# A decoder kernel's delta rule: query products made by GpSimd, VectorE's preparation in another order, first mixture's masked biases ahead of the sum

## What is computed

```python
for e in range(N_EXPERTS):
    h = jax.nn.relu(x @ W1[e] + b1[e])
    y = h @ W2[e] + b2[e]
    ff_out = ff_out + jnp.where((expert_idx == e)[..., None], y, 0.0)
return _layer_norm(x + ff_out, ln2_g, ln2_b)
```

```python
S = a_[..., None, None] * S
pred = jnp.einsum('bhkv,bhk->bhv', S, k_)
S = S + k_[..., :, None] * (b_[..., None] * (v_ - pred))[..., None, :]
o = jnp.einsum('bhkv,bhk->bhv', S, q_)
```

## Time and profile before

| | |
|---|---|
| median of 3 runs | 1845.26 us (1844.14 to 1848.06) |
| the profiled execution | 1845.25 us, span 1843.4 us |
| busy share of the span | TensorE 90%, VectorE 69%, ScalarE 52%, GpSimd 17% |
| mean granted TensorE clock | 0.957 of full speed |
| delta rule's preparation from k-hat to the scan | 1077.5 to 1127.4 us of the span |
| the scan | 1127.4 to 1311.5 us |

### The profile page before, as it was taken

The page is one execution under the profiler, slowest core; times in us unless marked ns, Lnnn a source line. Parts: engine busy times, 40 slices in busy tenths (PEclk is TensorE's granted clock), DMA queues, the critical chain, the costliest instruction groups (busy, mean ns, idle before and its releaser), DMA issues.

```text
span 1843.4 us, 24921 instructions
## 1 busy us (share of the span) xinstructions
PE 1653.6 (90%) x8074; PEld 736.0 (40%) x8074; DVE 1271.4 (69%) x2994; ACT 949.4 (52%) x2053; POOL 304.5 (17%) x465
## 2 busy tenths in 40 slices
PE   7899999999999989999899988444798899999998
PEld 3355455545544432222244331222443355444443
DVE  7576666767667768888565578999666677762423
ACT  3565556556645516666633566333236366664333
POOL 1000000000001021121277200000000222114443
PEclk9999999999999989999999999777799799999999
DMA  4000000000000220240000000000100512100000
GB/s 193 1 1 1 1 1 1 1 1 1 1 1 21 55 59 23 73 116 2 1 0 1 0 1 1 1 1 1 69 1 1 147 55 73 32 2 1 1 0 23
DMA packets 19806, 44.36 MB, mean 24 GB/s; under 512 B 3872, under 2 KB 13024, under 8 KB 18912
## 3 DMA queue, kind: packets, MB, share of 16 engines
q1 hardware_dynamic: 19200, 42.39, 7.6%
q10 hardware_dynamic: 480, 0.39, 0.1%
HBM read 32.74 MB, written 9.44 MB: 23 GB/s over the span
## 4 chain that ended last, share of the span: by engine, by line
PE 75%; DVE 16%; ACT 5%; issue 3%; POOL 1%; DMA 0%; ACTq 0%; POOLq 0%; SPq 0%; DVEq 0%
PE ps L675 8%; PE ps L639 8%; PE ps L653 6%; PE ps L1226 6%; PE ps L1264 5%; PE ps L1112 5%; PE ps L1699 3%; PE ps L1700 3%; PE ps L596 3%; PE ps L1596 3%; PE ps L1612 3%; PE ps L1707 3%; DVE arena L2063 2%; PE ps L684 2%; DVE arena L2050 2%
## 5 line engine op out<-in xcount | busy, mean ns | idle before, releaser
L1390 DVE TENSOR_REDUCE stat<-ps 128x1 f32<-128x512 f32 (+3 forms) x512 | 279.1, 581 | 86.6 <-PE ps L1116 43.0
L1321 ACT ACTIVATE arena<-ps 128x512 f32<-128x512 f32 (+3 forms) x512 | 247.1, 515 | 154.3 <-PE ps L1264 83.3
L826 DVE TENSOR_REDUCE stat<-ps 128x1 f32<-128x544 f32 x256 | 173.4, 719 | 163.0 <-PE ps L639 163.0
L777 ACT ACTIVATE arena<-ps,stat 128x544 f32<-128x544 f32 x256 | 180.7, 711 | 201.9 <-DVE stat L826 201.9
L1264 PE MATMUL ps<-arena 75*128 75x512 bf16 (+1 forms) x480 | 163.1, 344 | 11.7 <-ACT arena L1321 9.5
L1112 PE MATMUL ps<-arena 72*128 72x128 bf16 (+1 forms) x480 | 163.0, 348 | 8.0 <-DVE stat L1390 7.8
L675 PE MATMUL ps<-arena 128*64 128x512 f32 (+1 forms) x640 | 159.2, 609 | 4.7 <-DVE arena L845 3.3
L639 PE MATMUL ps<-arena 64*128 64x272 f32 x1024 | 152.1, 415 | 5.1 <-ACT arena L777 4.3
L785 ACT COPY arena<-ps 128x512 f32<-128x512 f32 x256 | 137.3, 594 | 15.5 <-PE ps L653 15.5
L653 PEld LDWEIGHTS ps<-wA_sb,arena 128*128 128x128 f32 x1024 | 115.1, 142 | 70.1 <-issue 68.9
L653 PE MATMUL ps<-wA_sb,arena 128*128 128x128 f32 x1024 | 138.3, 278 | 0.0
(11 more groups left out here) (391 smaller groups left out, 2775.2 us busy)
## 6 DMA issues: line engine op xcount, KB each, us to landing
arena<-b_parts SPq DMA_DIRECT2D x180, 96.0 KB
b_parts<-arena SPq DMA_DIRECT2D x64, 128.0 KB, 1.9
reg<-wM_dram SPq DMA_DIRECT2D x1, 3072.0 KB, 10.0
reg<-wB_dram SPq DMA_DIRECT2D x1, 2048.0 KB, 12.4
reg<-wM_dram SPq DMA_DIRECT2D x1, 2048.0 KB, 16.7
reg<-wD_dram SPq DMA_DIRECT2D x1, 1817.0 KB, 10.7
wF_sb<-wF_dram SPq DMA_DIRECT2D x1, 1476.0 KB, 19.8
reg<-b_parts SPq DMA_DIRECT2D x12, 96.0 KB
```

Of the source, the lines that this page charges most:

```text
L777: e.activation(prob_of(P, r).rearrange("p (a k) -> p a k", a=2), score_banks(r), ACT.Exp, bias=x_neg[:, at_:at_ + 1], accum_out=x_sums[:, ...
L826: e.tensor_reduce(x_neg[:, n % 4:n % 4 + 1], score_banks(r), AX.XY, ALU.max, negate=True).then_inc(sem("max_done"), 1)
L1321: e.activation(p_t[:, m % 8, q0:T], ps[:, S1 + m % S2, q0:T], ACT.Exp).then_inc(exp_done, 1)
L1390: e.tensor_reduce(nm[:, G % 2, u // 4, u % 4:u % 4 + 1], ps[:, step % S1, 0:keys(u)], AX.X, ALU.max, negate=True).then_inc(max_done, 1)
```

## The change

In the first mixture the four mask times bias additions come before the addition of the PSUM bank; they wait for the batch's last `up` instead of its last `down`.

In the preparation `g_ke`, `g_gq`, `g_pq[0]` and the query's six products for s = 1 to 3 are made by GpSimd (semaphore `b4_made`), which makes `g_ke` when k-hat is there and the others when q-hat is. VectorE forms `g_u` ahead of `g_z`, and q-hat behind the first of the three z and k pairs. The dots stand before the third `g_ke` pick (`KE_FIRST = 2`). `neg_delta` and the scratch of the solve get places of their own (`delta_flat`), so that k-hat and the places of the solve aren't overwritten. CB becomes 8: the `terms` buffers hold half as many blocks, and GpSimd fills 16 chunks instead of 8. VectorE waits for the last of GpSimd's products before it writes the part of `hist` that lies over alpha's second row (step 15).

```diff
--- before.py
+++ after.py
@@ -34,7 +34,7 @@
 PV_AT = 7
 BL = 4
 NB = T // BL
-CB = 16
+CB = 8
 NCB = NB // CB
 OUT = ((0, 32), (32, 32), (64, 32), (96, 16), (112, 16))
 OUT_OPS = 2 * 4 + BL
@@ -1634,15 +1634,13 @@
 
             def moe_dve(e):
                 def total(b):
+                    e.wait_ge(sem("moe_up"), (b + 1) * NI)
+                    e.wait_ge(sem("masks"), b + 1)
+                    for ex in range(E0):
+                        link(e, e.scalar_tensor_tensor(out=x_aux[:, b, :], in0=mask[:, b % 2, ex, :], scalar=v("f_b2", ex),
+                                                       in1=x_aux[:, b, :], op0=ALU.mult, op1=ALU.add))
                     e.wait_ge(sem("moe_down"), (b + 1) * NI)
-                    e.wait_ge(sem("masks"), b + 1)
-                    link(e, e.tensor_tensor(x_aux[:, b, :], ps[:, 4 + b % 2, :], x_aux[:, b, :], ALU.add))
-                    for ex in range(E0):
-                        i = e.scalar_tensor_tensor(out=x_aux[:, b, :], in0=mask[:, b % 2, ex, :],
-                                                   scalar=v("f_b2", ex), in1=x_aux[:, b, :], op0=ALU.mult, op1=ALU.add)
-                        if ex < E0 - 1:
-                            link(e, i)
-                    i.then_inc(sem("b3_sum"), 1)
+                    e.tensor_tensor(x_aux[:, b, :], ps[:, 4 + b % 2, :], x_aux[:, b, :], ALU.add).then_inc(sem("b3_sum"), 1)
                 masks(e, 1)
                 early_parts["last_total"](e)
                 early_parts["square"](e, B - 1)
@@ -1761,6 +1759,8 @@
             rank1 = slack[:, 0:64 * (BL + 1)].rearrange("p (a j d l) -> p a j d l", a=2, j=4, l=BL + 1)
             gamma = slack[:, 64 * (BL + 1):]
             g_k, g_q = c(B * T), c(B * T)
+            delta_flat = c(B * T)
+            neg_delta = delta_flat.rearrange("p (n i j) -> p n i j", i=BL, j=4)
             y = y_flat.rearrange("p (t w) -> p t w", w=12)
             k_end = k_end_flat.rearrange("p (t d) -> p t d", d=HD)
             hist = hist_flat.rearrange("p (n j d) -> p n j d", j=4, d=HD)
@@ -1770,7 +1770,7 @@
             M = B * NB
             flat = lambda x: x.rearrange("p b t -> p (b t)")
             g_alpha, g_beta = hist_flat[:, 0:BL * M], hist_flat[:, BL * M:2 * BL * M]
-            g_z, g_tmp = terms_flat[:, 0:BL * M], terms_flat[:, BL * M:BL * M + 3 * M]
+            g_z, g_tmp = terms_flat[:, 0:BL * M], delta_flat[:, 0:3 * M]
             g_pk, k_sq = y_flat[:, 0:6 * M], y_flat[:, 6 * M:10 * M]
             q_sq, g_to_end = k_end_flat[:, 0:B * T], k_end_flat[:, B * T:2 * B * T]
             qk = c(10 * M)
@@ -1785,7 +1785,6 @@
             def qk_of(s_):
                 return qk[:, PAIR0[s_] * M:(PAIR0[s_] + BL - s_) * M].rearrange("p (i b n) -> p b n i", i=BL - s_, b=B)
             q_wide = [x.rearrange("p b (n i) -> p b n i", i=BL) for x in (x_aux, cent)]
-            neg_delta = g_k.rearrange("p (n i j) -> p n i j", i=BL, j=4)
             o_prod = reg2[:, 0:8 * M].rearrange("p (a b t) -> p a b t", a=8, b=B)
             o_own = reg2[:, 8 * M:12 * M].rearrange("p (s b n i) -> p s b n i", s=BL, b=B, i=BL)
             PADW = CTAPS - 1
@@ -1798,10 +1797,11 @@
             PK0 = (None, 0, 3, 5)
             DOT0 = (0, 3, 5)
             PEB = 2
-            KE_FIRST = 5
+            KE_FIRST = 2
+            MADE = {x: n_ + 1 for n_, x in enumerate(("ke", "gq", "q0", "s1", "q1", "s2", "q2", "s3", "q3"))}
             GAMMA, KE, WW, UU, QK, GQ = 0, 1, 9, 17, 21, 31
             PICKS = 39
-            READY = {x: n_ + 1 for n_, x in enumerate(("gamma", "ke", "gq", "q0", "w", "u", "q1", "q2", "q3"))}
+            READY = {x: n_ + 1 for n_, x in enumerate(("gamma", "w", "u"))}
 
             def by_m(x, n_):
                 return x[:, 0:n_ * M].rearrange("p (i m) -> p i m", i=n_)
@@ -1865,7 +1865,7 @@
                     return lambda b: split_i(x)[:, :, b, :]
                 pick_k = [wt["pick_k"][:, d * 32:d * 32 + 32] for d in range(HD)]
                 pick_v = [wt["pick_v"][:, j * 32:j * 32 + 32] for j in range(4)]
-                e.wait_ge(sem("b4_ready"), READY["ke"])
+                e.wait_ge(sem("b4_made"), MADE["ke"])
                 e.wait_ge(sem("b4_ln"), 2 * B)
                 pick(GAMMA, pick_k[0], lambda b: split_i(g_gamma)[:, BL - 1, b, :])
                 for d in range(HD):
@@ -1889,7 +1889,7 @@
                     e.wait_ge(sem("b4_picked"), g - 1)
                     e.matmul(ps[:, 6 + g % 2, :], matrix, rhs, start=True, stop=True).then_inc(sem("b4_pick"), 1)
                 for s_ in range(BL):
-                    e.wait_ge(sem("b4_ready"), READY[f"q{s_}"])
+                    e.wait_ge(sem("b4_made"), MADE[f"q{s_}"])
                     for i in range(BL - s_):
                         wide(QK + PAIR0[s_] + i, wt["head_one"], g_pq[s_][:, i * M:i * M + M])
                 for a in range(2):
@@ -1981,13 +1981,11 @@
                     e.tensor_tensor(split_i(g_k)[:, :, b, :], tokens_by_i(ps[:, b:b + 1, :])[:, :, 0, :],
                                     split_i(r_k)[:, :, b, :], ALU.mult).then_inc(sem("b4_khat"), 1)
                 e.wait_ge(sem("b4_khat"), B)
-                e.wait_ge(sem("b4_ready"), READY["gamma"])
-                e.tensor_tensor(g_ke, g_k, g_to_end, ALU.mult).then_inc(sem("b4_ready"), 1)
                 e.wait_ge(sem("b4_act_read"), 2)
-                link(e, e.tensor_tensor(g_z, g_k, g_beta, ALU.mult))
                 e.wait_ge(sem("b4_proj"), 4 * B)
                 e.scalar_tensor_tensor(out=split_i(g_u), in0=tokens_by_i(ps[:, B:2 * B, :]), scalar=-1.0,
                                        in1=split_i(g_beta), op0=ALU.mult, op1=ALU.mult).then_inc(sem("b4_dve_read"), 1)
+                link(e, e.tensor_tensor(g_z, g_k, g_beta, ALU.mult))
                 e.wait_ge(sem("b4_ready"), READY["gamma"])
                 link(e, e.tensor_tensor(g_w, g_z, g_gamma, ALU.mult))
                 for s_ in range(1, BL):
@@ -1997,13 +1995,10 @@
                     w = (BL - s_) * M
                     e.tensor_tensor(g_pk[:, PK0[s_] * M:PK0[s_] * M + w], g_z[:, s_ * M:], g_k[:, 0:w],
                                     ALU.mult).then_inc(sem("b4_prod"), 1)
-                e.wait_ge(sem("b4_rlen"), 2 * B)
-                e.tensor_tensor(split_i(g_q), tokens_by_i(ps[:, 0:B, :]),
-                                split_i(r_q), ALU.mult).then_inc(sem("b4_dve_read"), 1)
-                e.wait_ge(sem("b4_dve_read"), 2)
-                e.wait_ge(sem("b4_ready"), READY["ke"])
-                e.tensor_tensor(g_gq, g_q, g_gamma, ALU.mult).then_inc(sem("b4_ready"), 1)
-                e.tensor_tensor(g_pq[0], g_q, g_k, ALU.mult).then_inc(sem("b4_ready"), 1)
+                    if s_ == 1:
+                        e.wait_ge(sem("b4_rlen"), 2 * B)
+                        e.tensor_tensor(split_i(g_q), tokens_by_i(ps[:, 0:B, :]),
+                                        split_i(r_q), ALU.mult).then_inc(sem("b4_dve_read"), 1)
                 e.wait_ge(sem("b4_prod"), BL - 1)
                 e.wait_ge(sem("b4_dot"), len(DOT0) * (len(DOT0) + 1) // 2)
                 for x in (g_w, g_u):
@@ -2018,14 +2013,6 @@
                             e.wait_ge(sem("b4_ready"), READY["w" if x is g_w else "u"])
                         else:
                             link(e, o)
-                for s_ in range(1, BL):
-                    w = (BL - s_) * M
-                    q_ = by_i(g_q)[:, s_:, :]
-                    link(e, e.tensor_tensor(q_, q_, a_[:, 1:BL + 1 - s_, :], ALU.mult))
-                    if s_ == 2:
-                        e.wait_ge(sem("b4_picked"), WW)
-                    e.tensor_tensor(g_pq[s_], g_q[:, s_ * M:], g_k[:, 0:w], ALU.mult).then_inc(sem("b4_ready"), 1)
-                    e.wait_ge(sem("b4_ready"), READY[f"q{s_}"])
                 e.memset(hist[:, 0, :, :], 0.0).then_inc(sem("b4_solved"), 1)
                 e.wait_ge(sem("b4_solved"), 1)
                 e.wait_ge(sem("b4_picked"), QK)
@@ -2035,7 +2022,9 @@
                     ch = n_ // CB
                     if n_ % CB == 0:
                         e.wait_ge(sem("b4_vset"), ch + 1)
-                    if n_ == 2 * CB:
+                    if n_ == BL * M // 128 - 1:
+                        e.wait_ge(sem("b4_made"), MADE["q3"])
+                    if n_ == OUT[0][1]:
                         e.wait_ge(sem("b4_picked"), PICKS)
                     slot = n_ % (2 * CB)
                     for a, js in enumerate(halves):
@@ -2118,6 +2107,22 @@
                         o = e.tensor_copy(terms[:, ch % 2 * CB:(ch % 2 + 1) * CB, i, :, HD],
                                           y[:, ch * CB * BL + i:(ch + 1) * CB * BL:BL, HD:12])
                     o.then_inc(sem("b4_vset"), 1)
+                a_ = by_i(g_alpha)
+                e.wait_ge(sem("b4_khat"), B)
+                e.wait_ge(sem("b4_ready"), READY["gamma"])
+                e.tensor_tensor(g_ke, g_k, g_to_end, ALU.mult).then_inc(sem("b4_made"), 1)
```

(12 more changed lines are left out.)

## The result

The changed kernel took 1852.98 us in the median of 6 executions, the kernel before 1844.7 beside it: a ratio of 1.0041, 95% interval 1.0027 to 1.0055, so 5 to 10 us slower. One execution of the first set took 6859.97 us, with TensorE's matmuls slow all through: the ratio is that of the other five (median 1852.21 us), and since it was the profiled one, all rows of the changed kernel are from e1, the same code again (span 1851.4 us, execution 1853.63 us).

A forecast was written before the change was run, and what follows sets the result against it. VectorE's queue up to g_q and the third product, then dots, solve and picks, were taken to bound the preparation. +8.2 - 0.7 - 0.6 + 0.1 = +7.0 us gave 1852.3 us, own range 1848.6 to 1855.8, 8 in 10: 1840 to 1856.

The forecast's parts named there:

- Turns and whole instructions (Part 2): Preparation: VectorE's two-SBUF instructions wait for whole GpSimd products, 4.2 us beside 2048 columns; g_w 8.2 us later.
- the low end of the range: Lower bound of GpSimd's hold per column, 1.91 to 2.23 ns, making g_w 7.1 to 9.5 us later.
- that rival: Preparation: GpSimd gives way inside long products, each wait 0.6 to 1 us; 1843.1 us, no change; chance 0.13.
- the rival without blocking: Preparation: VectorE goes first or runs beside GpSimd, so the new order's gain stands; -8.5 us, 1836.8 us; chance 0.17.
- The last dot: TensorE in the preparation, after the third product (1107.5): 0.9 us for a dot, done by 1108.5, 6.0 later than before.
- The end of `g_w`: Last subtraction of the solve on VectorE: at 1118.3, 8.2 us later than the 1110.1 before.
- my sequence: Preparation: step-by-step turns of VectorE and GpSimd in the trace's clock, from ke at 1077.6 to g_w at 1118.3.
- From `g_w` to the scan: Picks before the scan: 17.3 us, less 0.7 (0 to 1.5) because TensorE stands idle less before them.
- k-hat to scan in all: Preparation up to the scan: g_w +8.2 us and the quicker picks -0.7.
- A reading of the kernel before: Preparation: the dots wait for g_q, ending 1096.3, since it frees their PSUM banks.
- The mixture (Part 3): First mixture: last batch's sum 1.95 us earlier, worth -0.6 us (0.2 to 1.95); nothing for the other three batches.
- The copies (Part 4): Scan: GpSimd's 64 copies of 32 columns instead of 32 of 64, +0.1 us in all (-0.3 to +1.3).

The follow-up runs named there:

- e1: The changed kernel unchanged, run again for an undisturbed profile: 1853.66 us, 1.0045 of the kernel before.
- e3: Against the changed kernel, each of GpSimd's products cut into instructions of 512 columns: 1845.13 us, 0.9999 of the kernel before.
- e2: Against the changed kernel, GpSimd's nine products replaced by two memsets each, products left out of the computation: 1838.35 us, 0.9967 of the kernel before.
- e11: The kernel before once more, nothing changed: 1845.94 us against 1844.46 of the same code beside it, 1.0014.
- e10: VectorE's new order; GpSimd makes only g_ke and g_gq, in 512-column pieces under PSUM-reading instructions; repeated on another kernel's chip: 1840.05 us, 0.9977 of the kernel before.
- e8: Against the changed kernel, VectorE makes the products, except g_ke and g_gq on GpSimd in 512-column pieces under PSUM-reading instructions: 1839.69 us, 0.9970 of the kernel before.

## Why the prediction was right

1852.3 us was forecast and 1852.98 measured, by the mechanism named. That the two are so close is in part luck: the stages that the change touches got 5.6 us longer, not 7.0, and the total has some 2 us more that no stage of the prediction holds (see the end of this section). Step by step:

- *Turns and whole instructions (Part 2).* Right. The wait was taken as 4.2, 3.1 and 2.0 us for 2048, 1536 and 1024 columns: measured 5.41 - 1.23 = 4.18 and 4.87 - 0.69 = 4.18 beside 2048, 3.79 - 0.69 = 3.10 beside 1536. `g_z` waited 2.02 (1.9). GpSimd's products of 2048 and 512 columns, 4.54 and 1.28 us, make 2.12 ns for each further column, where 2.1 was taken; the 1.91 at the low end of the range has no row behind it (the prediction's own rows give 1.95 at least). What waits of at most 1 us would have made is e3, 1845.1 us against 1843.1 forecast for that rival; the rival without blocking was e2, 1838.4 against 1836.8 forecast.
- *The last dot.* 0.9 us were taken, it took 2.08: TensorE had waited 5.06 us for the third product and started at the lower clock. The granted clock from 1107.6 to 1109.7 was 0.50:

```profile
1107.60 2.08 PE L1878 MATMUL ps<-arena,reg 128*128 128x512 f32 x2 [5.06 <-DVE arena L1996]
```

```profile
1107.60:1109.70 2.10, 2.10 (x6) 0.60 (x10) 0.00 (x0) 0.00 (x0) 2.10 (x1) 0.50 0.00 0
```

- *The end of `g_w`.* Forecast 1118.3, measured 1118.86. Inside, two errors cancel. Because of the late dot the first subtraction came at 1111.58, when GpSimd's s2 had begun (1110.92), and waited 1.56 us instead of 0.3. The second and third waited for nothing, where my sequence had some 2 us: GpSimd's q2 (L2124) hung on `b4_picked`, that is on ScalarE's evictions of the `g_ke` picks (idle 5.44), which the sequence had left out.
- *From `g_w` to the scan.* Forecast 17.3 - 0.7, measured 15.3: TensorE had been idle for 1.39 us before these picks, where it was 4.43 in the kernel before, and ran them at a granted clock of 1.00, where the kernel before had 0.51 over its first 5 us of them (1110 to 1115). So the whole 1.5 us and some more came back.
- *k-hat to scan in all:* forecast +8.2 - 0.7 = +7.5, measured +6.9 (+6.7 against e11).
- *A reading of the kernel before.* The prediction says that the dots wait there for q-hat, which ends at 1096.3. They start at 1097.07, when the fifth `g_ke` pick is done (1096.01, 1.07 us, behind an eviction of ScalarE); q-hat was there 0.7 us earlier. The forecast doesn't hang on it, since `KE_FIRST = 2` puts the dots ahead of those picks.
- *The mixture (Part 3).* Forecast -0.6, measured -1.4 in the profiles. For the last batch it was as forecast: counted from the end of the last `down` the sum ends 2.3 us sooner than before (1.95 forecast; it is at 1030.93 in e1, where the last `down` ends 0.4 us later), but L211 starts only 0.3 us sooner, idle 1.68 for ScalarE's root, and k-hat comes 0.5 us nearer the last `down` (0.6 forecast). What failed is the sentence that for the other three batches an earlier sum is worth nothing. In the kernel before the biases lay beside the next batch's first gatings (GpSimd's first took 1.63 us, in e1 1.26); the first `down` of that batch came late. Timeline of TensorE in the kernel before, then in e1:

```profile
973.33 3.60 PE L1612 MATMUL ps<-x_aux,reg 128*128 128x512 f32 x8
976.90 1.13 PE L1596 MATMUL ps<-reg 128*128 128x512 f32 x2
977.87 1.02 PE L1612 MATMUL ps<-x_aux,reg 128*128 128x512 f32 x2
```

```profile
974.29 3.60 PE L1612 MATMUL ps<-x_aux,reg 128*128 128x512 f32 x8
977.73 1.02 PE L1596 MATMUL ps<-reg 128*128 128x512 f32 x2
978.59 1.02 PE L1612 MATMUL ps<-x_aux,reg 128*128 128x512 f32 x2
```

  From the first of these rows to the last it is 4.54 us, then 4.30, so 0.24 at this border; there are three, which would make 0.7 of the 0.86 us by which the mixture is shorter (116.14, now 115.28). It fits the same blocking, which I had used for GpSimd's products and which the change relieves here; no run tests that by itself.
- *The copies (Part 4).* Forecast +0.1, less than any run could show; the scan is 0.2 to 0.3 us longer, within what the same code differs by. Eight of GpSimd's copies of 32 columns take 1.30 us where the earlier trace rows have 1.53 for eight of 64.

The Trainium skill ("SBUF — State Buffer", section Who interferes with whom) says that VectorE with two SBUF inputs contends with a GpSimd instruction that reads SBUF, not with one that only writes. e1 and e2 show both halves: 4.18 us of waiting beside a product, none beside a memset of the same tile. It also says that the loser is blocked for the whole instruction, and e1 against e3 shows that (4.18 us beside 2048 columns, 0.95 beside 512).

What stays open: the stages explain +5.6 to +5.7 us, and the two ratios put the total at +7.6 (5.0 to 10.1) and +8.3 (5.9 to 10.7), so the second interval leaves the stages' sum just out. Two things on record bear on it. The profiled executions of e1 and e11 had the same mean granted TensorE clock, 0.954, and their spans differ by 5.6 us, which is the stages' sum. And all six executions of e1 had 0.954, while those of the kernel before beside it had 0.954 to 0.962; the five of them at 0.954 took 1847.0 to 1849.0 us, median 1847.5, which is 6.2 below e1's. So the rest goes with the clock over the whole span. Whether the change itself lowers that clock outside its own stages is not shown. It could: other kernels with the change's parts also gained less in the total than in these stages (e2 6.1 to 7.0 of 10.1 us, e3 0.2 of 1.8, e10 some 4.3 of 6.0, but e8 5.5 of 5.9), and no run isolates why.

## What to carry to other kernels

Before work goes to an idle GpSimd, look at what VectorE does at that time: beside instructions with two SBUF inputs each GpSimd product that reads SBUF costs VectorE up to its whole length, and here the blocking cost 15.6 us (e2 against e1) where the work taken off VectorE and its new order were worth 8.7 (e2 against before). It was free beside instructions that read PSUM (e8), or where GpSimd only writes (e2); cut the product to fit under them, and release each piece by a semaphore. And if TensorE stands idle before a short burst on the critical path, look at its granted clock in the burst: here 3.5 us of idle time made 5.6 us of dots into 8.1.

## What the runs showed of the hardware

- The blocking goes both ways, by who comes second. In e3 g_z took its 2.28 us undisturbed, and GpSimd's piece of `g_ke` that met it took 3.3 us instead of 1.28 (durations in ns, min/median/max):

```profile
L2114 POOL TENSOR_TENSOR reg<-arena x6: 1276/1280/3322, 1075.5 to 1120.2; 128x512 f32<-128x512 f32 x6
```

- While VectorE is the one that waits, GpSimd's product of 2048 columns takes 4.54 us (L2113), one of 512 columns 1.28.
- Four matmuls whose result nobody reads brought the scan 2.4 us nearer to k-hat (45.3, then 42.9), since the six dots that followed 3.5 us of idle time ran at a granted clock of 0.66 otherwise (8.13 against 5.56 us).
- VectorE's waiting for GpSimd counts as busy: its busy time went from 1271.4 to 1273.5 us although 14 us of its work went to GpSimd.
